# A three-layer feature-interaction tower with a dense top: first loads, weight splits and waits in another order, rows of ones loaded by DMA, dense rows stacked under the first z tile

## What is computed

```python
h = e
for i, (W, bias) in enumerate(params):
    x = einsum('bhd,bmd->bhmd', h, e).reshape(B, -1, D)
    y = relu(einsum('oi,bid->bod', W, x) + bias[None, :, None])
    if i != 2:
        h, direct = split(y, 2, axis=1)
    else:
        direct = y
    outs.append(direct)
z = concatenate(outs, axis=1).sum(-1)
h = concatenate([z, dense_ctx], axis=1)
h = relu(h @ W_top1 + b_top1)
h = relu(h @ W_top2 + b_top2)
y = h @ W_top3
```

## Time and profile before

| | |
|---|---|
| median of 3 runs | 2904.6 us (2903.6 to 2905.39) |
| the profiled execution's own time | 2907.22 us |
| its span | 2905.5 us |
| TensorE matmul busy | 2830.5 us, 97% of the span |
| VectorE busy | 2607.7 us, 90% |
| ScalarE busy | 1502.0 us, 52% |
| GpSimd busy | 688.1 us, 24% |
| mean granted TensorE clock | 0.993 |

### The profile page before, as it was taken

The page is one execution under the profiler, slowest core; times in us unless marked ns, Lnnn a source line. Parts: engine busy times, 40 slices in busy tenths (PEclk is TensorE's granted clock), DMA queues, the critical chain, the costliest instruction groups (busy, mean ns, idle before and its releaser), DMA issues.

```text
span 2905.5 us, 54782 instructions
## 1 busy us (share of the span) xinstructions
PE 2830.5 (97%) x19516; PEld 2811.0 (97%) x19516; DVE 2607.7 (90%) x1751; ACT 1502.0 (52%) x1880; POOL 688.1 (24%) x669
## 2 busy tenths in 40 slices
PE   2899999999999999999999999999999999999998
PEld 2899999999999999999999999999999999999996
DVE  4899999999999999999999999999999999999993
ACT  2555555555555555555555555555555555555552
POOL 2122222222222222222222222222222222222000
PEclk8999999999999999999999999999999999999999
DMA  6434333334333334333334334334333334334320
GB/s 158 101 67 100 86 74 97 86 74 98 87 74 96 87 74 99 87 74 97 87 75 98 86 74 97 87 75 96 89 73 96 88 75 99 87 75 94 95 57 21
DMA packets 280089, 249.92 MB, mean 86 GB/s; under 512 B 27803, under 2 KB 278602, under 8 KB 279965
## 3 DMA queue, kind: packets, MB, share of 16 engines
q1 hardware_dynamic: 211192, 196.57, 23.8%
q0 software_dynamic: 59744, 45.90, 11.0%
q10 hardware_dynamic: 9129, 7.13, 1.0%
HBM read 140.44 MB, written 4.20 MB: 50 GB/s over the span
## 4 chain that ended last, share of the span: by engine, by line
PE 96%; DMA 1%; SPq 1%; DVE 1%; issue 1%; ACT 0%; POOL 0%; DVEq 0%; ACTq 0%; POOLq 0%
PE acc L717 62%; PE acc L719 29%; PE z_ps L734 3%; PE hid_ps L730 1%; SPq L349 1%; PE acc L777 0%; DMA x_pairs<-x_rows 0%; DVE product L660 0%; DMA raw_weights<-in_w 0%; DVE tails L665 0%; PE hid_ps L800 0%; SPq L321 0%; DMA hid_rep<-hid 0%; POOL gathered L410 0%; DMA starts_sb<-in_table_starts 0%
## 5 line engine op out<-in xcount | busy, mean ns | idle before, releaser
L717 PE MATMUL acc<-weights,heads 126*128 126x400 f32 (+1 forms) x9088 | 2707.9, 365 | 62.3 <-DVE tails L665 62.3
L719 PE MATMUL acc<-weights,tails 126*128 126x200 f32 (+1 forms) x9088 | 2324.3, 256 | 0.0
L484 ACT ACTIVATE heads<-product 126x1024 fp32r<-126x1024 f32 (+2 forms) x1152 | 1203.9, 1048 | 1149.9 <-PE acc L719 749.5
L717 PEld LDWEIGHTS acc<-weights,heads 126*128 126x128 f32 (+1 forms) x9088 | 1717.0, 189 | 63.8 <-issue 46.6
L719 PEld LDWEIGHTS acc<-weights,tails 126*128 126x128 f32 (+1 forms) x9088 | 1744.7, 192 | 0.0
L660 DVE TENSOR_TENSOR product<-hid_rep,x_rep 126x2048 f32<-126x2048 f32 x512 | 1172.5, 2290 | 214.8 <-PE acc L719 175.5
L665 DVE TENSOR_TENSOR tails<-product,heads 126x1024 fp32r<-126x1024 f32 (+2 forms) x1152 | 1338.4, 1203 | 3.4 <-ACT heads L484 3.4
L418 POOL TENSOR_TENSOR wait_taker<-wait_taker 1x1 f32<-1x1 f32 x192 | 106.8, 556 | 2069.0 <-ACT acc_copy L490 2067.3
L410 POOL DMA_INDIRECT gathered<-in_table,rows_now x150 | 316.5, 2110 | 45.7 <-issue 45.7
L495 ACT ACTIVATE y_relu<-acc_copy 128x400 f32<-128x400 f32 x192 | 102.4, 533 | 192.8 <-DMA acc_copy<-acc_copy 192.8
L419 POOL DMA_DIRECT2D acc_copy<-acc_copy x192 | 175.8, 916 | 1.1 <-issue 0.6
(11 more groups left out here) (27 smaller groups left out, 106.4 us busy)
## 6 DMA issues: line engine op xcount, KB each, us to landing
x_rep<-x_rows SPq DMA_DIRECT2D x512, 120.0 KB
hid_rep<-hid SPq DMA_DIRECT2D x512, 120.0 KB
x_pairs<-x_rows SPq DMA_DIRECT2D x192, 280.0 KB
acc_copy<-acc_copy POOLq DMA_DIRECT2D x192, 200.0 KB
hid_rep<-hid SPq DMA_DIRECT2D x512, 5.0 KB
x_pairs<-x_rows SPq DMA_DIRECT2D x64, 120.0 KB
raw_weights<-in_w ACTq DMA_DIRECT2D x12, 492.2 KB
x_rep<-x_rows SPq DMA_DIRECT2D x128, 20.0 KB
```

What stands on the lines that cost most here:

```text
L484: act.activation(heads[0:rows, ring % HEADS_RING, 0:tiles, :], product[0:rows, ring % PRODUCT_RING, 0:tiles, :], ACT.Copy).then_inc(heads_ ...
L717: nc.tensor.matmul(acc[:, at.parity, c, 0:2 * LAYER], heads[0:rows, ring % HEADS_RING, k, cols], w, start=(q == 0 and k == 0), stop=False)
L719: last = nc.tensor.matmul(acc[:, at.parity, c, LAYER:2 * LAYER], tails[0:rows, ring % PRODUCT_RING, k, cols], w[:, 0:LAYER], start=False, ...
```

## The change

The ids carry the table starts as one more column, so one load brings both. The rows of ones come by four DMAs of SyncE, and VectorE's memsets go. Five weight loads instead of four are issued at the start, the other four of layer 1 right behind the split of chunk 1, three of layer 2 in step 1 behind both heads of layer 0, and each split of layer 2 then issues the load three chunks ahead. Chunks 2 to 4 are split at the start, 5 to 8 in step 0, 9 and 10 in step 1 behind layer 0, the rest one per two groups from there. ScalarE's relu of block 0 comes behind both heads of block 1. On SyncE the second half of the first load_x_rep and the second store come behind the pairs of block 1. load_hid has four DMAs of 25 maps, and its two halves have a semaphore each; products wait for the half that they read. The dense rows of the top layer lie in rows 100 to 115 of z's first part. Cut to its core:

```diff
-EARLY_LOADS = 4
+EARLY_LOADS, AHEAD_LOADS = 5, 3
+W1_FIRST, W2_FIRST = 3, 2
...
-        z_t = sb("z_t", [HALF, Q_PARTS, batch])
+        z_t = sb("z_t", [HALF + DENSE, Q_PARTS, batch])
...
-        HID_DMAS = 2 * HID_OUT
-        CONSTS = 7
+        HID_PART = HID_OUT // 2
+        CONSTS = 6
...
             if i == "start":
-                return list(range(split_until[0]))
+                return list(range(split_until[0])) + w1[:W1_FIRST]
             if (i, layer) == (0, 0):
-                return w1[:4]
+                return w1[W1_FIRST:]
             if (i, layer) == (1, 0):
-                return w1[4:]
+                return w2[:W2_FIRST]
             if layer == 1 and i in (1, 2):
-                n = (i - 1) * (GROUPS // 2) + q // 2
+                n = W2_FIRST + (i - 1) * (GROUPS // 2) + q // 2
                 return w2[n:n + 1]
...
             sp.dma_start(rows_all[:, :, :], ids).then_inc(ids_loaded, 16)
-            sp.dma_start(starts_sb[:, :], table_starts).then_inc(ids_loaded, 16)
...
+            for row in (x_pairs[PAIRS0:PAIRS0 + 1, :, :], x_rep[PAIRS:PAIRS + 1, :, :, :],
+                        hid_rep[0][PAIRS:PAIRS + 1, :, :], hid_rep[1][PAIRS:PAIRS + 1, :, :]):
...
+                sp.dma_start(flat, ones_in[:, 0:flat.shape[1]]).then_inc(ones_loaded, 16)
...
-            sp.wait_ge(ones_set, 1)
             load_pairs(0, 0)
-            sp.wait_ge(ones_set, 2)
-            for half in range(FLD_HALVES):
-                load_x_rep(0, 0, half)
-            sp.wait_ge(x_gathered, GATHERS)
-            store(1)
-            sp.wait_ge(ones_set, 3)
+            load_x_rep(0, 0, 0)
 
             def load_hid(n):
                 for g in range(HID_OUT):
-                    for rows, first, maps in ((slice(0, MAIN), 0, HID_MAIN), (slice(MAIN, PAIRS), HID_MAIN, 1)):
-                        at = g * HID_IN + first
-                        sp.dma_start(hid_rep[n][rows, g, :],
-                                     hid[n][at:at + maps, :].unsqueeze(1).to_broadcast([maps, FLD_IN, COLS])).then_inc(hid_loaded[n], 16)
+                    maps = hid[n][g * HID_IN:(g + 1) * HID_IN, :]
+                    sp.dma_start(hid_rep[n][0:PAIRS, g, :],
+                                 maps.unsqueeze(1).to_broadcast([HID_IN, FLD_IN, COLS])).then_inc(hid_loaded[n][g // HID_PART], 16)
...
                     load_pairs(duo, 1 + parity)
+                if not whole and i == 0:
+                    load_x_rep(0, 0, 1)
+                    sp.wait_ge(x_gathered, GATHERS)
+                    store(1)
+                    sp.wait_ge(prep_added, 2)
...
-                    if n in split_after(0, 0) or n > split_until[1]:
-                        load_weights(n + 1 + EARLY_LOADS)
+                    if n == split_until[0] - 1:
+                        load_weights(split_until[1])
+                    if n >= split_until[1]:
+                        load_weights(n + 1 + AHEAD_LOADS)
...
                     make_heads(*l0, 0)
+                    make_heads(*l0, 1)
+                    load_weights(split_until[1] + AHEAD_LOADS)
                     relu(*before)
-                    make_heads(*l0, 1)
                     copy_turned(*before)
...
-            dve.memset(x_pairs[:, :, :], 1.0).then_inc(ones_set, 1)
-
-            dve.wait_ge(ids_loaded, 16 * 2)
+            dve.wait_ge(ids_loaded, 16)
...
-            dve.memset(x_rep[:, :, :, :], 1.0).then_inc(ones_set, 1)
...
-            dve.wait_ge(prep_added, 2)
-            dve.memset(hid_rep[0][:, :, :], 1.0)
-            dve.memset(hid_rep[1][:, :, :], 1.0).then_inc(ones_set, 1)
...
-                    if q == 0:
-                        dve.wait_ge(hid_loaded[layer - 1], (b + 1) * (16 * HID_DMAS))
+                    if q < HID_OUT:
+                        dve.wait_ge(hid_loaded[layer - 1][hid_block // HID_PART], (b + 1) * (16 * HID_PART))
...
-            dve.wait_ge(ones_set, 3)
+            dve.wait_ge(ones_loaded, 16 * 4)
...
-                if q == 0 and isinstance(b, int) and b == 0:
-                    pe.wait_ge(weight_tails, split_until[layer])
+                if isinstance(b, int) and b == 0:
+                    pe.wait_ge(weight_tails, split_until[0] + q - 1 if layer == 0 else
+                               split_until[layer - 1] + (GROUP * q + GROUP - 1) // PREP_TILES + 1)
...
-                if not end:
-                    nc.tensor.matmul(bank, wt1d_sb[:, cols], dense_sb[:, :], start=True, stop=False)
                 for q in parts:
-                    last = nc.tensor.matmul(bank, wt1z_sb[:, q, cols], z_t[:, q, :],
-                                            start=False, stop=(q == Q_PARTS - 1))
+                    rows = HALF + DENSE if q == 0 else HALF
+                    last = nc.tensor.matmul(bank, wt1z_sb[0:rows, q, cols], z_t[0:rows, q, :],
+                                            start=(q == 0), stop=(q == Q_PARTS - 1))
```

More of the change, by code:

```diff
@@ L69, with cin_kernel @@
 PREP_TILES = 5
-EARLY_LOADS = 4
+EARLY_LOADS, AHEAD_LOADS = 5, 3
+W1_FIRST, W2_FIRST = 3, 2
 Q_PARTS = 4
 Place = namedtuple("Place", "group ring slot parity")
-def cin_kernel(nc, ids, table_starts, table, w0a, w0b, w1, w2, dense_t, wt1z, wt1d, wt2, wt3, bt1, bt2,
-               ident_in, sum32_in, out):
-    duos = ids.shape[1]
+def cin_kernel(nc, ids, table, w0a, w0b, w1, w2, dense_t, wt1z, wt1d, wt2, wt3, bt1, bt2,
+               ident_in, sum32_in, ones_in, out):
+    duos = ids.shape[1] - 1
     batch = duos * DUO
@@ L150, in cin_kernel @@
         bt2_sb = sb("bt2_sb", [128, TOP2 // 128])
-        wt1z_sb = x_pairs[0:HALF, :, :].rearrange("p a c -> p (a c)").rearrange(
+        wt1z_sb = x_pairs[0:HALF + DENSE, :, :].rearrange("p a c -> p (a c)").rearrange(
             "p (q n) -> p q n", q=Q_PARTS)
@@ L170, in cin_kernel @@
         weight_tails = sem("weight_tails")
-        ones_set = sem("ones_set")
+        ones_loaded = sem("ones_loaded")
         rows_ready = sem("rows_ready")
@@ L182, in cin_kernel @@
         x_rep_loaded = [[sem(f"x_rep_loaded{p}{h}") for h in range(FLD_HALVES)] for p in range(2)]
-        hid_loaded = [sem("hid_loaded1"), sem("hid_loaded2")]
+        hid_loaded = [[sem(f"hid_loaded{n}{half}") for half in range(2)] for n in (1, 2)]
         products_made = sem("products_made")
@@ L501, in copy_turned @@
                 if layer < 2:
-                    above_zero(act, hid_loaded[layer], b * (16 * HID_DMAS))
+                    for half in range(2):
+                        above_zero(act, hid_loaded[layer][half], b * (16 * HID_PART))
                     act.activation(hid[layer][:, :], hid_ps[0:HALF, layer, 0:COLS], ACT.Copy).then_inc(hid_copied[layer], 1)
-                    act.activation(z_t[:, layer, cols], z_ps[0:HALF, at.parity, 0:BLOCK], ACT.Copy).then_inc(z_copied, 1)
+                    act.activation(z_t[0:HALF, layer, cols], z_ps[0:HALF, at.parity, 0:BLOCK], ACT.Copy).then_inc(z_copied, 1)
                 else:
-                    act.activation(z_t[:, 2:4, cols],
+                    act.activation(z_t[0:HALF, 2:4, cols],
                                    z_ps[0:HALF, at.parity, 0:2 * BLOCK].rearrange("p (q b) -> p q b", q=2),
@@ L543, in step @@
                     make_heads(*l0, 1)
-                    if odd is None and i == 0:
-                        load_weights(split_until[0] + EARLY_LOADS)
                     split_heads(*(split_after(i, 0, 0) if odd is None else ()))
@@ L553, in step @@
                     make_heads(*first, q)
-                if odd is None and i == 1:
-                    load_weights(split_until[1] + 1 + EARLY_LOADS)
                 if before:
@@ L610, in _ @@
         def _(dve):
[L612 to L617 removed]
+            dve.wait_ge(ids_loaded, 16)
+            dve.tensor_tensor(rows_all[:, 0:duos, :], rows_all[:, 0:duos, :],
+                              rows_all[:, duos:duos + 1, :].to_broadcast([128, duos, FLD_DMA]), ALU.add).then_inc(rows_ready, 1)
             def split_tails(*chunks_now):
@@ L829, in lay_out @@
     ids = arr("ids").reshape(batch // DUO, DUO, FLD_DMA, FLD_PART).transpose(3, 1, 0, 2)
-    packed = {"ids": np.ascontiguousarray(ids.reshape(128, batch // DUO, FLD_DMA)), "w0a": w0a, "w0b": w0b}
+    ids = ids.reshape(128, batch // DUO, FLD_DMA)
+    packed = {"w0a": w0a, "w0b": w0b}
     for n in (1, 2):
@@ L850, in lay_out @@
     starts = np.cumsum([0] + [t.shape[0] for t in tables[:-1]]).astype(np.int32)
-    packed["table_starts"] = np.repeat(starts.reshape(FLD_DMA, FLD_PART).T, DUO, axis=0)
+    starts = np.repeat(starts.reshape(FLD_DMA, FLD_PART).T, DUO, axis=0)
+    packed["ids"] = np.ascontiguousarray(np.concatenate([ids, starts[:, None, :].astype(ids.dtype)], axis=1))
+    packed["ones"] = np.ones((1, 2 * FLD_OUT * COLS), np.float32)
     return packed
@@ L861, in build @@
     out = nc.dram_tensor("out_y", (batch, 1), F32, kind="ExternalOutput").ap()
-    cin_kernel(nc, args["ids"], args["table_starts"], args["table"], args["w0a"], args["w0b"], args["w1"],
```

(3 more changed lines are left out.)

17 lines of the change are left out of this document (7 added, 10 removed).

## The result

The change made the kernel slower: 3028.48 us (3005.55 to 3041.38, 4 runs) against 2904.99 (2903.6 to 2905.82, 4 runs), ratio 1.0417 [1.0349, 1.0485]. The forecast was 2881.6, with 2870 to 2893 as its range. The profiled execution took 3036.06 us, its span is 3034.3, 128.8 more than before's.

The account below looks back on a forecast made before the run. TensorE bounds the loop; its 72.8 us of idle stretches at the two ends, and low clock behind them, can be won. Terms sum to 23.0: 2884.2 for the profiled execution, median 2881.6 from 2904.6, range 2870 to 2893.

Parts of the forecast that it names:

- in a loop where TensorE is the bound: nothing: Loop: added weight waits on TensorE and hid semaphore waits on VectorE and ScalarE were priced at nothing.
- the case in which they hold up relu: Loop, rival "Slower": summing DMA 1.5 us late beside merged hid loads, 0.7 lost per block, +42, total 2924; chance 0.05.
- Start: First idle stretch: ids 2.1 us earlier, early weight loads costing 1.1; -1.0, between -3.8 and +4.
- Most of the free time comes before 20.43: Opening: reason for pricing the early weight loads at 1.1 us, within 0 to 6.1.
- x_rep, store and relu: Second idle stretch: second product at 42.4, relu at 47.5, ScalarE's order late last; -4.0, between -6 and +2.
- Third stretch: Opening's third TensorE idle stretch: hid halves let the product come sooner; -1.5, between -2.7 and +2.
- hid in halves: Opening and end: a half takes 5.1 us from first issue to product; saves 3.0 at the end, 2.7 early.
- Fourth and fifth: Opening's idle stretches: fourth -4.3, between -6.4 and -2, as chunk 12 comes ahead; fifth -2.7 by hid halves.
- Sixth: Idle stretch of 1.90 us goes by hid halves, with 1.8 of low clock behind it; -3.7.
- Seventh: Idle stretch near the end: hid halves shorten it, its low clock stays; -3.0.
- Dense rows: Kernel's end: four dense matmuls go, two hidden but for 0.7 us, two on the path, 2.1; -2.8.

Follow-up runs that it names:

- 24 and 1 maps: Changed kernel with each part's hid load split again into DMAs of 24 maps and 1 map, halves kept: 2891.02 us, ratio 0.9946 against the kernel before.
- 25-map loads at twice the spacing: Changed kernel with a small unread load of one map behind each 25-map load, eight issues again: 2917.43 us, ratio 1.0032 against the kernel before.
- the held x_rep: Changed kernel, 25-map loads, the first half of x_rep in the loop waiting for all products of layer 2: 3008.73 us, 1.0341 against the kernel before.
- the later loads: 24 and 1 maps, one load fewer at the start, chunks 4 to 8 loaded behind block 0's heads: 2891.1 us, 0.9944 against the kernel before.
- the cover at the top: 24 and 1 maps plus two unread matmuls ahead of the top layer's last turn: 2895.16 us, 0.9956 against the kernel before.

## Why the prediction was wrong

**The step that failed** is the price of the merged hid loads in the loop. The prediction took them for a matter of the two ends: its sum has no term for them in the loop, which it closed with "in a loop where TensorE is the bound: nothing" (said of the semaphores, where it held), and it gave the case in which they hold up relu 0.05. Its argument against that case was that TensorE shows no idle time though the summing DMA already comes 2 us late. TensorE was the bound with a slack of 0.8 us, on a DMA that was already what relu waited for; a bound with so small a slack is no cover. The rival's place and mechanism are what happened: five engines' share, the summing DMA late, relu late, TensorE idle. Its size was off. It took the DMA 1.5 us late and 0.7 us lost per block, 42 in all; measured are 7.8 us from issue to relu instead of 5.5, 2.3 us late (median), 1.45 lost per wait and 82 of idle time. It also left out the clock, 48.7 us more, although stood beside it. And its argument against itself, that merged loads need half as many issues, points the other way: with 25 maps, the quick pace of those four issues makes 111 of the 137 us (3028 against 2917).

**The rest of the change** can be read from 24 and 1 maps: -17.2 us between the profiled executions (2889.99 against 2907.22), where 23.0 were forecast. By steps:

- *Start*: forecast -1.0; after +5.3, 24 and 1 maps +2.6 (37.19 against 34.63). The maps play no part so early: 37.19 is the least and 39.91 the most of the eight profiles with this opening. The sign was wrong. The gather's 2.0 us did come, and were lost beside the weights. "Most of the free time comes before 20.43" was the failing choice: four of the five moved loads held ScalarE's queue for 7.65 us, from 11.86 on, just where gathers, store and pairs run. The upper bound, +4, was passed in after.
- *x_rep, store and relu*: forecast -4.0; the second stretch is 8.81 against 10.51, -1.7 (9.89, -0.6, with 24 and 1 maps). The product came 11.5 us behind the first, near the forecast 12.3, but relu waits 4.14 for the summing DMA: the sum is late last, not ScalarE's order. It took 7.3 us from the copy's end (47.55) to relu where 3.6, the end's, was taken.
- *Third stretch*: forecast -1.5; +2.0 after, 0 with 24 and 1 maps (6.95). From hid's first issue to the product the half takes 10.5 us here and 8.1 there, where 5.1 was worked out (with 6.49 for eight, 0.81 an issue and not 0.83, it is 5.0). Three weight loads are issued from 56.70 on, just ahead of hid, and "hid in halves" was priced at the end's rate, where none run; that they are what slows it is argued, no run shows it alone.
- *Fourth and fifth*: forecast -4.3 and -2.7; measured -4.1 (2.38 against 6.43) and -2.4 (2.28 against 4.66). Right, and for the reason given: chunk 12 is there, and in the fourth VectorE works without a pause.
- *Sixth*: the 1.90 went, as forecast.
- *Seventh*: 5.5 us from issue to product (2969.32 to 2974.84) against 5.1 worked out; the stretch is 5.19 against 7.77, -2.6 where -3.0 was forecast (-3.5 with 24 and 1 maps, 4.29).
- *Dense rows*: forecast -2.8; 24 and 1 maps give 3.0 from the last copy to the end (27.2 against 30.17 in before, whose copy is the row below). After gives 1.3, since there the clock fell behind the wait that the two removed matmuls had covered.

```profile
2875.33 0.84 ACT L490 ACTIVATE acc_copy<-acc 128x800 f32<-128x800 f32 x1 [8.92 <-PE acc L719]
```

So the profiled execution is 151.8 us off the forecast (+128.8 where -23.0 was expected). Of these 134.6 lie in the loop, where its -3.7 came to +130.9, 14.3 in the opening (+0.8 where -13.5 was expected) and 2.9 at the end. With 24 and 1 maps only 5.8 us of the 23.0 are missing, all in the opening, where loads that move out of one wait come to lie beside another: TensorE leaves the fifth stretch at 94.94 instead of 101.55, 6.6 us sooner where 13.5 were expected.

## What to carry to other kernels

Fewer and larger DMAs aren't cheaper as such: look at the DMA share while the loads run alone, and keep the count of a broadcast's slowest dimension such that the share is high. In a loop without idle time, list the waits that end just ahead of the bound engine and their slack; an edit that delays one of them by less than that costs nothing, and one that delays it by more is paid in every block, and again in the clock. In an opening whose idle stretches have a DMA share of up to 0.9, as here, moving a load only pays where nothing urgent runs beside it.

## What was not expected of the hardware

- The pace of issues decides as much as their shape: 25-map loads at twice the spacing lost 26 us against 24 and 1 maps, and back to back 137 (2917 and 3028 against 2891).
- The same 12.46 us for GpSimd's one-element operation stood in the profiles of the held x_rep, the later loads and the cover at the top, against 0.43 in that of 24 and 1 maps. The Trainium skill (SBUF — State Buffer, Who interferes with whom) says that a VectorE instruction with two inputs in the on-chip memory contends with a GpSimd instruction that reads it, not with one that only writes. The runs agree: read 12.46, write 0.09. The section, of the two-port modes, has the first hold the shared ports for its whole instruction, and mostly the reading operation got in behind one (1.30 us at most in the rest of that trace); here it waited through ten of VectorE's, 71.75 to 84.17. What makes it miss nine gaps is open.
- A wait of 0.93 us left TensorE's clock at 1.00, one of 2.72 left 0.62 and 0.52 for 4 us, and one of 1.62 cost the clock in one execution only.
